# Cross-attentions: probabilities turned on four 32-row tiles in two rounds, shifting score banks, division behind the values

## The chip, the cores and the metric

The kernel runs on one core of a Trainium2 chip. The metric is device time in microseconds from launch to end of the whole decoder, the median of several executions. All matrices are float32.

## What is computed

A decoder of four layers, each with a self-attention, a cross-attention and a feed-forward part, on 8 sequences of 56 tokens with 256 features. The cross-attentions of layers 0, 2 and 3 have 16 heads and attend to a context of 1500 positions per sequence with 64 features. The part of the reference that matters here:

```python
        scores = jnp.einsum('bhsr,bhlr->bhsl', q_r, k_r)
        attn = jax.nn.softmax(scores, axis=-1)
        ctx_c = jnp.einsum('bhsl,bld->bhsd', attn, kv_r)
        ctx_lat = jnp.einsum('bhsd,hkd->bhsk', ctx_c, w_kc_kv)
        ctx = ctx_lat.transpose(0, 2, 1, 3).reshape(Bv, Sv, H * K)
        return ctx @ Wo.T
```

## The kernel before

`cross_attention` is called three times. Ahead of its loop it folds the weights so that a query has 64 features, like the context. Then it walks over `NU` = 28 units: 4 pairs of sequences (`j`) times 7 groups (`u`) of 128 rows, a row being one head of one token. A unit holds 128 rows for each sequence of the pair (`e` = 0, 1) and goes through these steps:

- **Scores** (`score(i, k)`, L1035): the 128 x 1500 scores of both sequences, in three parts of 500 columns. Sequence 0 uses rows 0 to 63 of the array, sequence 1 rows 64 to 127, so two 64-row tiles run at once. They land in PSUM banks 0 to 2 (`e` = 0) and 3 to 5 (`e` = 1). A float32 matmul is issued as two.
- **Softmax**: VectorE takes the row maxima (`rowmax`: L1315 for the three parts of sequence 0, L1320 for sequence 1 at once), ScalarE takes the exponential and the sum in one pass (`exp`, L1236), VectorE inverts the sum (L1324) and multiplies the 128 x 1500 probabilities by it in SBUF (`divide`, L1328), once per sequence.
- **Turning** (`turn(i, k)`, L1122): TensorE transposes the probabilities in blocks of 125 columns, 24 blocks a unit (12 per sequence). Each block is two transposes, of rows 0 to 63 and 64 to 127, into two banks; the block is the stationary operand, a 64 x 64 identity moves. Eight blocks fill a pair of banks; so there are three rounds `k`. The banks are those that the scores of the next unit, already exponentiated, have left, and banks 6 and 7. Two banks are copied by VectorE (L1334), four by ScalarE (L1243), 512 columns each.
- **Weighing** (`weigh(i)`, L1135): the turned probabilities times the context, summed over 12 blocks, into bank 6. VectorE copies the 128 x 128 values out (`keep`, L1341), GpSimd places them (L908).
- **Projection** (`project(j)`, L1150), after the loop.

The order on TensorE is written out: in step `i` come the scores of unit `i`, the weighing of unit `i-2`, the turning of unit `i-1`. All waits are written by hand on semaphores; every engine works its own list in order. TensorE's waits in `score` protect the banks that `turn` of the unit before last has filled and the copies have to empty (`d_in` counts VectorE's copies, `a_in` ScalarE's); those in `turn` wait for the exponentials that free the score banks (`exped`) and for the divided probabilities (`normed`).

TensorE's list, as it stands:

```python
        for i in range(1, NU):
            for k in range(3):
                score(i, k)
...
            if i >= 2:
                weigh(i - 2)
            for k in turn_order(i - 1):
                turn(i - 1, k)
```

Of the kernel before, what the change touches and what calls it, by code (L numbers as in the profile page):

```python
# [16 lines left out]
ALU = mybir.AluOpType  # L17
# [747 lines left out]
def cross_attention(c, name, o, rope, now, prefetch):  # L765
# [5 lines left out]
    s.y, s.turn_at, s.idle_bank, s.order = [(0, 0), (0, 1), (1, 0), (4, 0)], (2, 3, 5, 7), 6, range(J)  # L771
# [13 lines left out]
    else:  # L785
# [20 lines left out]
    pT = [c.at(o["PT"] + i * LT * 256, LT * 256, LP).rearrange("p (r s q) -> p r s q", r=2, q=64) for i in range(2)]  # L806
    probs = [[c.at(o["P"] + (2 * i + e) * L, L) for e in range(2)] for i in range(2)]
    held = [c.at(o["RB"] + 128 * i, 128) for i in range(2)]
    low, total, inv = (c.sb_small[:, 8 * n:8 * n + 8].rearrange("p (i e) -> p i e", e=2) for n in range(3))
    peak = c.sb_small[:, 24:36].rearrange("p (i k) -> p i k", k=3)  # L810
    sc = [c.ps[:, 3 * e:3 * e + 3, 0:4 * LP] for e in range(2)]
# [5 lines left out]
    scored, lowered, exped, recip, normed = (  # L817
        [s.sem(x + "_%d" % e) for e in range(2)] for x in ("scored", "lowered", "exped", "recip", "normed"))
    maxed, turned_lo, turned_hi, d_in, a_in, pv_mm, kept, ct_in, ct_last = (
        s.sem(x) for x in ("maxed", "turned_lo", "turned_hi", "d_in", "a_in", "pv_mm", "kept", "ct_in", "ct_last"))  # L820
# [8 lines left out]
    def turn_bank(i, k, r):  # L829
# [16 lines left out]
    def score_order(i):  # L846

        return (2, 1, 0) if i == 0 else (0, 1, 2)

    def turn_order(i):  # L850

        return (2, 0, 1) if i == 0 else (0, 1, 2)
# [37 lines left out]
    def _(pool):  # L890
# [21 lines left out]
    def _(pe):  # L912
# [108 lines left out]
        def score(i, k):  # L1021

            if i == 0 and k < 2:
                pe.wait_ge(cm_act.handle, cm_act.at(2 - k))
            if i > 0 and k == 0:
                for e in range(2):
                    pe.wait_ge(exped[e].handle, exped[e].at(i))
            if i > 1 and k < 2:
                pe.wait_ge(d_in.handle, d_in.at(2 * (i - 2) + 1 + k))
            if i > 1 and k == 2:  # L1030
                pe.wait_ge(a_in.handle, a_in.at(4 * (i - 2) + 3))
            j, u = i // UNITS, i % UNITS
            q = q2[:, j, :, :].rearrange("p h t -> p (h t)")[:, u * 128:(u + 1) * 128]
            for e in range(2):
                m = nc.tensor.matmul(sc[e][:, k, :], q[e * 64:(e + 1) * 64],  # L1035
# [4 lines left out]
                elif k == score_order(i)[-1]:  # L1040
                    m.then_inc(*scored[1].next())

        if rope:
# [22 lines left out]
            for k in score_order(0):  # L1066
                if k == 0:
                    pe.wait_ge(prod3_in.handle, prod3_in.at(3 * NH // 2))
                score(0, k)
            third(NH // 2 - 1)  # L1070
        else:
            for t in range(8):
# [17 lines left out]
                if t == 6:  # L1090
# [5 lines left out]
                    for k in score_order(0):  # L1096
                        score(0, k)
# [6 lines left out]
        def turn(i, k):  # L1104

            if k == turn_order(i)[0]:
                for e in range(2):
                    pe.wait_ge(normed[e].handle, normed[e].at(i + 1))
            if k == 0 and i < NU - 1:
                pe.wait_ge(exped[0].handle, exped[0].at(i + 2))  # L1110
            if k == 2 and i > 0:
                pe.wait_ge(kept.handle, kept.at(i))
            if i == 0 and k == 2:
                pe.wait_ge(lat_in.handle, lat_in.at(4 * NH // 2))
                pe.wait_ge(cm_act.handle, cm_act.at(3))
            if k == (1 if i == 0 else 2) and i < NU - 1:
                pe.wait_ge(exped[1].handle, exped[1].at(i + 2))
            for n in range(8):
                e, l = divmod(8 * k + n, LT)
                for r in range(2):  # L1120
                    rows = slice(r * 64, (r + 1) * 64)
                    m = nc.tensor.transpose(c.ps[0:LP, turn_bank(i, k, r), n * 64:(n + 1) * 64],  # L1122
                                            probs[i % 2][e][rows, l * LP:(l + 1) * LP], c.ident[rows, rows])
                    if n == 7:
                        m.then_inc(*(turned_hi if r else turned_lo).next())

        def weigh(i):

            j, u = i // UNITS, i % UNITS
            pe.wait_ge(a_in.handle, a_in.at(4 * (i + 1)))  # L1130
            pe.wait_ge(d_in.handle, d_in.at(2 * (i + 1)))
            y = c.ps[:, 6, :]
            for l in range(LT):
                for r, e, lo, hi in parts(u):
                    m = nc.tensor.matmul(y[r * 64:(r + 1) * 64, lo:hi], c.ctx_pos[:, j, l, e, :],  # L1135
                                         pT[i % 2][:, lo // 64:hi // 64, LT * e + l, :], start=(l == 0 and lo == 0),
# [18 lines left out]
        for i in range(1, NU):  # L1155
            for k in range(3):
                score(i, k)
            if i == 1:

                pe.wait_ge(cm_act.handle, cm_act.at(3))  # L1160
                keep_busy(c, 6, 1)
                keep_busy(c, 6, 1, None, 256)
            if i >= 2:
                weigh(i - 2)
            for k in turn_order(i - 1):
                turn(i - 1, k)
        pe.wait_ge(d_in.handle, d_in.at(2 * (NU - 1)))
# [3 lines left out]
        for k in range(3):  # L1171
            turn(NU - 1, k)
# [13 lines left out]
    def _(act):  # L1186
# [45 lines left out]
        def exp(i, e):  # L1232
            act.wait_ge(lowered[e].handle, lowered[e].at(i + 1))
            if i == 0 and not rope:
                act.wait_ge(wide_in.handle, wide_in.at(4))
            nc.scalar.activation(probs[i % 2][e].rearrange("p (k l) -> p k l", k=3), sc[e],  # L1236
                                 ACT.Exp, bias=low[:, i % 4, e:e + 1],
                                 accum_out=total[:, i % 4, e:e + 1]).then_inc(*exped[e].next())

        def copy_turned(i, k, r):  # L1240
# [1774 lines left out]
```

## Time and profile before

| | |
|---|---|
| median of 3 runs | 1663.95 us (1662.07 to 1665.45) |
| the profiled execution, its span | 1666.3 us |
| TensorE matmuls busy | 1627.4 us, 98% |
| VectorE busy | 1113.9 us, 67% |
| ScalarE busy | 749.9 us, 45% |
| GpSimd busy | 239.1 us, 14% |

In the profile PE is TensorE's matmuls and PEld its weight loads, which overlap; DVE is VectorE, ACT ScalarE, POOL GpSimd. L1122 is line 1122 of the kernel. The three unit loops lie at 205 to 456, 827 to 1077 and 1336 to 1586 us of the span. A matmul's recorded duration contains its way through the array, so several overlap; the distance between starts is what one costs.

### The profile page before, as it was taken

What the parts mean: (1) busy time and instruction counts of PE and PEld (TensorE: products, weight loads), DVE (VectorE), ACT (ScalarE), POOL (GpSimd) and SP (SyncE); (2) the same over time, 40 slices, a digit from 0 to 9 for tenths busy, and PEclk for the clock granted to TensorE, in tenths of its full rate; (3) what the DMA queues carried; (4) which work ended last, traced back from release to release, by engine and by line L of the source; (5) the groups of instructions that cost most, each with busy time, mean ns of one, the idle gap of its engine ahead of it and who ended that gap; (6) DMA issues with size and microseconds to landing.
All of it is one profiled execution on the core that took longest, in us unless ns stands there. A gap on an engine that the chain in (4) does not pass through costs nothing.

```text
span 1666.3 us, 35653 instructions
## 1 busy us (share of the span) xinstructions
PE 1627.4 (98%) x15234; PEld 1104.8 (66%) x15234; DVE 1113.9 (67%) x1974; ACT 749.9 (45%) x1297; POOL 239.1 (14%) x428
## 2 busy tenths in 40 slices
PE   9999999999999899999999999999999999999998
PEld 5575367777755666655377777764566767777765
DVE  3735899999566763266899999435445289999623
ACT  2223366666413641144366666312444366666411
POOL 0011300000010313011200000010455000000030
PEclk9999999999999999999999999999999999999999
DMA  8302020000040011051020000050300220000010
GB/s 280 86 13 83 1 78 2 2 2 2 2 187 1 2 59 40 1 133 48 1 97 2 2 2 2 4 240 0 64 1 1 114 89 2 2 2 2 2 44 11
DMA packets 35522, 71.10 MB, mean 43 GB/s; under 512 B 25359, under 2 KB 29775, under 8 KB 31433
## 3 DMA queue, kind: packets, MB, share of 16 engines
q1 hardware_dynamic: 35240, 68.71, 12.6%
q8 instruction: 121, 1.98, 0.5%
q14 instruction: 35, 0.29, 0.1%
q10 hardware_dynamic: 126, 0.11, 0.0%
HBM read 68.36 MB, written 0.46 MB: 41 GB/s over the span
## 4 chain that ended last, share of the span: by engine, by line
PE 89%; DVE 6%; ACT 2%; POOL 1%; issue 1%; DMA 1%; SPq 0%; DVEq 0%; POOLq 0%; ACTq 0%
PE ps L1122 14%; PE ps L1135 14%; PE ps L1035 13%; PE ps L1501 9%; PE ps L361 9%; PE ps L946 3%; PE ps L2599 3%; PE ps L1150 3%; PE ps L528 2%; PE ps L1961 2%; PE ps L956 1%; POOL arena L1795 1%; PE ps L2626 1%; PE ps L982 1%; PE ps L967 1%
## 5 line engine op out<-in xcount | busy, mean ns | idle before, releaser
L1236 ACT ACTIVATE arena<-ps,softmax_stats 128x1500 f32<-128x1500 f32 x168 | 253.8, 1511 | 193.0 <-DVE softmax_stats L1317 190.8
L1135 PEld LDWEIGHTS ps<-arena,ctx_pos 125*64 125x64 f32 x4608 | 222.3, 137 | 58.4 <-issue 55.4
L1122 PE MATMUL ps<-ident,arena 64*125 64x64 f32 x4032 | 239.1, 271 | 1.9 <-ACT arena L1236 1.6
L1135 PE MATMUL ps<-arena,ctx_pos 125*64 125x128 f32 (+1 forms) x4608 | 240.5, 262 | 0.0
L1122 PEld LDWEIGHTS ps<-ident,arena 64*125 64x125 f32 x4032 | 226.8, 185 | 17.0 <-issue 13.5
L1035 PE MATMUL ps<-ctx_feat,arena 64*128 64x500 f32 x1008 | 230.5, 590 | 0.0
L1243 ACT COPY arena<-ps 125x512 f32<-125x512 f32 x336 | 172.5, 600 | 77.9 <-PE ps L1122 77.9
L1315 DVE TENSOR_REDUCE softmax_stats<-ps 128x1 f32<-128x500 f32 x252 | 170.6, 678 | 49.0 <-PE ps L1035 48.6
L361 PE MATMUL ps<-arena 128*128 128x256 f32 x736 | 174.7, 383 | 3.5 <-DVE arena L1630 1.2
L1328 DVE TENSOR_SCALAR arena<-arena,softmax_stats 128x1500 f32<-128x1500 f32 x168 | 168.3, 1002 | 5.9
L1501 PE MATMUL ps<-x_feat,arena 128*128 128x448 f32 (+1 forms) x416 | 167.9, 549 | 1.2 <-DVE arena L1613 1.2
L361 PEld LDWEIGHTS ps<-arena 128*128 128x128 f32 x736 | 137.0, 190 | 40.9 <-issue 16.6
L908 POOL COPY arena<-arena 64x128 f32<-64x128 f32 (+1 forms) x186 | 51.1, 275 | 682.6 <-DVE arena L1341 676.5
L1320 DVE TENSOR_REDUCE softmax_stats<-ps 128x1 f32<-128x1500 f32 x84 | 143.6, 1709 | 0.0
L1035 PEld LDWEIGHTS ps<-ctx_feat,arena 64*128 64x128 f32 x1008 | 89.2, 187 | 80.0 <-issue 77.1
L1501 PEld LDWEIGHTS ps<-x_feat,arena 128*128 128x128 f32 (+1 forms) x416 | 79.3, 193 | 65.7 <-issue 61.7
L1334 DVE COPY arena<-ps 125x512 f32<-125x512 f32 x168 | 107.6, 682 | 12.8 <-PE ps L1122 12.5
L1577 ACT ACTIVATE arena<-ps 128x448 f32<-128x448 f32 (+1 forms) x52 | 28.2, 543 | 187.0 <-PE ps L1501 187.0
L1613 DVE TENSOR_TENSOR arena<-ps,arena 128x448 f32<-128x448 f32 x41 | 25.6, 624 | 115.6 <-ACT arena L1577 87.9
L946 PE MATMUL ps<-x_feat,arena 128*128 128x448 f32 x128 | 56.1, 563 | 0.2
L2599 PE MATMUL ps<-x_feat,arena 128*128 128x448 f32 x128 | 52.4, 552 | 1.2 <-issue 0.7
L2727 DVE TENSOR_TENSOR arena<-ps,arena 128x448 f32<-128x448 f32 x32 | 20.0, 625 | 46.0 <-ACT arena L2671 45.9
(324 smaller groups left out, 1931.7 us busy)
## 6 DMA issues: line engine op xcount, KB each, us to landing
ctx_pos<-in_ctx SPq DMA_DIRECT2D x1, 2688.0 KB
arena<-in_L1f_gate SPq DMA_DIRECT2D x1, 2304.0 KB, 12.1
arena<-in_L1f_up SPq DMA_DIRECT2D x1, 2304.0 KB, 17.0
arena<-in_L1f_down SPq DMA_DIRECT2D x1, 2304.0 KB, 7.8
arena<-in_L0a_Wq SPq DMA_DIRECT2D x1, 2048.0 KB, 10.9
arena<-in_L0a_Wc SPq DMA_DIRECT2D x1, 2048.0 KB, 18.8
arena<-in_L0x_Wq SPq DMA_DIRECT2D x1, 2048.0 KB, 9.9
arena<-in_L0x_Wo SPq DMA_DIRECT2D x1, 2048.0 KB, 8.3
```

The lines of the kernel that those rows point to most:

```text
L361: m = c.nc.tensor.matmul(y_of(c, s, j), lhsT, rhs, start=False, stop=last, skip_group_check=True)
L946: m = nc.tensor.matmul(c.ps[:, 2 + h % 2, 0:NT], wq[:, k, h, :], c.x_feat[:, k, :, 0:T], start=(k == 0), stop=(k == KT - 1))
L1035: m = nc.tensor.matmul(sc[e][:, k, :], q[e * 64:(e + 1) * 64], c.ctx_feat[e * 64:(e + 1) * 64, j, k * 4 * LP:(k + 1) * 4 * LP], start=True ...
L1122: m = nc.tensor.transpose(c.ps[0:LP, turn_bank(i, k, r), n * 64:(n + 1) * 64], probs[i % 2][e][rows, l * LP:(l + 1) * LP], c.ident[rows, r ...
L1135: m = nc.tensor.matmul(y[r * 64:(r + 1) * 64, lo:hi], c.ctx_pos[:, j, l, e, :], pT[i % 2][:, lo // 64:hi // 64, LT * e + l, :], start=(l = ...
L1236: nc.scalar.activation(probs[i % 2][e].rearrange("p (k l) -> p k l", k=3), sc[e], ACT.Exp, bias=low[:, i % 4, e:e + 1], accum_out=total[:, ...
L1243: nc.scalar.copy(pT[i % 2][:, r, 8 * k:8 * k + 8, :], c.ps[0:LP, turn_bank(i, k, r), :].rearrange("p (s q) -> p s q", s=8)).then_inc(*a_in ...
L1315: nc.vector.tensor_reduce(peak[:, i % 4, k:k + 1], sc[0][:, k, :], AX.X, ALU.max).then_inc(*maxed.next())
L1320: nc.vector.tensor_reduce(low[:, i % 4, 1:2], sc[1], AX.XY, ALU.max, negate=True).then_inc(*lowered[1].next())
L1328: nc.vector.tensor_scalar(probs[i % 2][e], probs[i % 2][e], inv[:, i % 4, e:e + 1], None, ALU.mult).then_inc(*normed[e].next())
L1334: nc.vector.tensor_copy(pT[i % 2][:, r, 0:8, :], c.ps[0:LP, turn_bank(i, 0, r), :].rearrange("p (s q) -> p s q", s=8)).then_inc(*d_in.next())
L1501: m = nc.tensor.matmul(c.ps[0:m_, bank(n) + i, 0:NT], w[:, k, n * 128:n * 128 + m_], c.x_feat[:, k, :, 0:T], start=(k == 0), stop=(k == KT ...
```

## The change

- **Turning**: for units 1 to 26 all 24 blocks go as four transposes of 32 rows each, into four banks (32 columns a block). Round 0 has 16 blocks (four banks of 512 columns), round 1 has 8 (four of 256). Unit 0 keeps 64-row tiles in three rounds; the last unit has a round of 16 blocks on four tiles and one of 8 on two. VectorE copies two banks of round 0 and one of round 1, ScalarE the other two and three.
- **Banks**: the scores of sequence 1 lie in banks 3 to 5 for even units and 4 to 6 for odd ones, their order within the unit changes, and the values go to bank 7. The waits in `score` follow the new copies.
- **Division**: the probabilities aren't divided. GpSimd spreads the two inverses of a row over 128 columns (`widen`), TensorE transposes that into a spare bank ahead of weighing (`spread_inverse`; for the middle unit of seven four small matmuls), ScalarE copies it out (`copy_inverse`), and VectorE multiplies by it where it copied the values before (`keep`, `keep_last`).

The core of the diff:

```diff
-    pT = [c.at(o["PT"] + i * LT * 256, LT * 256, LP).rearrange("p (r s q) -> p r s q", r=2, q=64) for i in range(2)]
+    pT = [c.at(o["PT"] + i * LT * 256, LT * 256, LP).rearrange("p (s q) -> p s q", q=128) for i in range(2)]
...
+    def first_bank(i, e):
+        return (3 + i % 2) * e
...
+    def spare(i):
+        return 6 if i % 2 == 0 else 3
+    def rounds(i):
         if i == 0:
-            return ((0, 1), (2, 5), (6, 7))[k][r]
+            return [(0, 8, (3, VALUES)), (8, 8, (0, 1)), (16, 8, (2, 6))]
         if i == NU - 1:
-            return ((2, 3), (4, 7), (6, 5))[k][r]
-        return ((0, 1), (2, 7), (6, 5))[k][r]
+            return [(0, 16, (2, 3, 5, 6)), (16, 8, (4, VALUES))]
+        if i % 2 == 0:
+            return [(0, 16, (0, 3, 1, 2)), (16, 8, (4, 5, VALUES, 6))]
+        return [(0, 16, (0, 6, 1, 2)), (16, 8, (4, 5, VALUES, 3))]
+    def inv_bank(i):
+        return spare(i + 2) if i + 2 < NU else 4
...
+        def widen(i):
+            pool.wait_ge(recip.handle, recip.at(i + 1))
+            nc.gpsimd.tensor_copy(wide_inv[i % 2].rearrange("p (s d) -> p s d", s=2),
+                                  inv[:, i % 4, :].unsqueeze(2).broadcast_to([128, 2, 64])).then_inc(*widened.next())
+        widen(0)
         for i in range(NU - 1):
+            if i > 0:
+                pool.wait_ge(ct_in.handle, ct_in.at(placed(i - 1)))
+            widen(i + 1)
+            pool.wait_ge(widened.handle, widened.at(i + 2))
...
-            if i > 0 and k == 0:
+        def score(i, n):
+            if i == 0 and n > 0:
+                pe.wait_ge(cm_act.handle, cm_act.at(n))
+            if i > 0 and n == 0:
                 for e in range(2):
                     pe.wait_ge(exped[e].handle, exped[e].at(i))
-            if i > 1 and k < 2:
-                pe.wait_ge(d_in.handle, d_in.at(2 * (i - 2) + 1 + k))
-            if i > 1 and k == 2:
-                pe.wait_ge(a_in.handle, a_in.at(4 * (i - 2) + 3))
+            if i == 1 and n == 2:
+                pe.wait_ge(cm_act.handle, cm_act.at(3))
+            if i == 2 and n < 2:
+                pe.wait_ge(d_in.handle, d_in.at(d_at(0, n + 1)))
+            if i == 2 and n == 2:
+                pe.wait_ge(a_in.handle, a_in.at(a_at(0, 3)))
+            if i > 2:
+                pe.wait_ge(d_in.handle, d_in.at(d_at(i - 2, (1, 3, 3)[n])))
+                pe.wait_ge(a_in.handle, a_in.at(a_at(i - 2, (1, 1, 3)[n])))
...
+        def turn(i, n):
+            if i == 0 and n == 0:
+                pe.wait_ge(lat_in.handle, lat_in.at(4 * NH // 2))
+            if i < NU - 1 and n == (1 if i == 0 else 0):
                 pe.wait_ge(exped[0].handle, exped[0].at(i + 2))
-            if k == 2 and i > 0:
+            if i > 0 and n == 0:
+                pe.wait_ge(inv_in.handle, inv_in.at(i))
+            if i > 0 and n == 1:
                 pe.wait_ge(kept.handle, kept.at(i))
-            if i == 0 and k == 2:
-                pe.wait_ge(lat_in.handle, lat_in.at(4 * NH // 2))
-                pe.wait_ge(cm_act.handle, cm_act.at(3))
-            if k == (1 if i == 0 else 2) and i < NU - 1:
+            if i < NU - 1 and n == len(rounds(i)) - 1:
                 pe.wait_ge(exped[1].handle, exped[1].at(i + 2))
-            for n in range(8):
-                e, l = divmod(8 * k + n, LT)
-                for r in range(2):
-                    rows = slice(r * 64, (r + 1) * 64)
-                    m = nc.tensor.transpose(c.ps[0:LP, turn_bank(i, k, r), n * 64:(n + 1) * 64],
+            block, blocks, banks = rounds(i)[n]
+            w = 128 // len(banks)
+            for m in range(blocks):
+                e, l = divmod(block + m, LT)
+                for t, bank in enumerate(banks):
+                    rows = slice(t * w, (t + 1) * w)
+                    x = nc.tensor.transpose(c.ps[0:LP, bank, m * w:(m + 1) * w],
                                             probs[i % 2][e][rows, l * LP:(l + 1) * LP], c.ident[rows, rows])
-                    if n == 7:
-                        m.then_inc(*(turned_hi if r else turned_lo).next())
+                    if m == blocks - 1:
+                        x.then_inc(*turned[t].next())
+        def spread_inverse(i):
+            u = i % UNITS
+            pe.wait_ge(widened.handle, widened.at(i + 1))
+            if u == SPLIT:
+                for r, e, lo, hi in parts(u):
+                    m = nc.tensor.matmul(c.ps[r * 64:(r + 1) * 64, inv_bank(i), lo:hi], inv[:, i % 4, e:e + 1].broadcast_to([128, 64]),
+                                         c.ident[:, lo:hi], start=True, stop=True, skip_group_check=True)
+            else:
+                m = nc.tensor.transpose(c.ps[:, inv_bank(i), 0:128], wide_inv[i % 2], c.ident[:])
+            m.then_inc(*inv_mm.next())
...
+            pe.wait_ge(a_in.handle, a_in.at(a_at(i, a_copies(i))))
+            pe.wait_ge(d_in.handle, d_in.at(d_at(i, d_copies(i))))
+            spread_inverse(i)
...
+                copy_inverse(i - 2)
             if i < NU:
                 exp(i, 0)
                 exp(i, 1)
             if i == 0:
                 cm_out(3)
                 place(7)
-            if i >= 1:
-                copy_turned(i - 1, 1, 0)
-                copy_turned(i - 1, 1, 1)
-                copy_turned(i - 1, 2, 1)
-                copy_turned(i - 1, 2, 0)
+            if i == 1:
+                copy_turned(0, 0, 0)
+                copy_turned(0, 0, 1)
+                copy_turned(0, 2, 0)
+                copy_turned(0, 2, 1)
+            if i >= 2:
+                copy_turned(i - 1, 0, 1)
+                copy_turned(i - 1, 0, 3)
+                if i < NU:
+                    copy_turned(i - 1, 1, 1)
+                    copy_turned(i - 1, 1, 2)
+                    copy_turned(i - 1, 1, 3)
...
-        def divide(i, e):
-            dve.wait_ge(recip[e].handle, recip[e].at(i + 1))
-            nc.vector.tensor_scalar(probs[i % 2][e], probs[i % 2][e], inv[:, i % 4, e:e + 1], None,
-                                    ALU.mult).then_inc(*normed[e].next())
...
+            nc.vector.tensor_tensor(held[i % 2], c.ps[:, VALUES, 0:128], spread[i % 2], ALU.mult).then_inc(*kept.next())
...
+                copy_turned(i - 1, 0, 0)
+                copy_turned(i - 1, 0, 2)
+                if i < NU:
+                    copy_turned(i - 1, 1, 0)
             if i < NU:
-                normalise(i, 1)
+                invert(i)
```

## Rows read from the trace of the kernel before

**Rows 1.** The page: span, busy times of two engines, the turning's group.

```profile
span 1666.3 us, 35653 instructions
...
PE 1627.4 (98%) x15234; PEld 1104.8 (66%) x15234; DVE 1113.9 (67%) x1974; ACT 749.9 (45%) x1297; POOL 239.1 (14%) x428
...
L1122 PE MATMUL ps<-ident,arena 64*125 64x64 f32 x4032 | 239.1, 271 | 1.9 <-ACT arena L1236 1.6
```

**Rows 2.** The page: lines of the chain that ended last, share of the span.

```profile
PE ps L1122 14%; PE ps L1135 14%; PE ps L1035 13%; PE ps L1501 9%; PE ps L361 9%; PE ps L946 3%; PE ps L2599 3%; PE ps L1150 3%; PE ps L528 2%; PE ps L1961 2%; PE ps L956 1%; POOL arena L1795 1%; PE ps L2626 1%; PE ps L982 1%; PE ps L967 1%
```

**Rows 3.** Busy times by engine inside the first loop; columns in the first line.

```profile
core 0: us, PE busy (x) PEld busy (x) DVE busy (x) ACT busy (x) POOL busy (x), PEclk, DMA share, GB/s
300.00:400.00 100.00, 100.00 (x1432) 78.08 (x1432) 91.94 (x150) 64.93 (x101) 8.23 (x30) 1.00 0.01 2
```

**Rows 4.** Order of time, one unit: start us, us; then engine, line, operation, count.

```profile
334.35 2.73 PE L1035 MATMUL ps<-ctx_feat,arena 64*128 64x500 f32 x12
...
337.01 2.60 PEld L1135 LDWEIGHTS ps<-arena,ctx_pos 125*64 125x64 f32 x48 [0.74 <-issue]
...
339.43 0.19 ACT L1236 ACTIVATION_READ_ACCUMULATOR arena<-ps,softmax_stats 128x1 f32 x1
...
339.78 2.69 PEld L1122 LDWEIGHTS ps<-ident,arena 64*125 64x125 f32 x48 [0.17 <-issue]
...
340.97 1.28 DVE L1334 COPY arena<-ps 125x512 f32<-125x512 f32 x2
...
341.77 2.05 ACT L1243 COPY arena<-ps 125x512 f32<-125x512 f32 x4 [0.53 <-PE ps L1122]
...
342.39 0.30 PEld L1035 LDWEIGHTS ps<-ctx_feat,arena 64*128 64x128 f32 x4
342.45 2.73 PE L1035 MATMUL ps<-ctx_feat,arena 64*128 64x500 f32 x12
```

**Rows 5.** Order of time, TensorE: the unit's last pair of score matmuls.

```profile
336.50 0.58 PE L1035 MATMUL ps<-ctx_feat,arena 64*128 64x500 f32 x2
```

**Rows 6.** Single lines, weight loads: duration ns minimum/median/maximum; shape.

```profile
L967 PEld LDWEIGHTS ps<-arena x128: 106/108/109, 149.4 to 822.7; 128*32 128x32 f32 x128
...
L924 PEld LDWEIGHTS ps<-arena x192: 156/162/162, 142.4 to 1304.6; 64*96 64x96 f32 x192
...
L1122 PEld LDWEIGHTS ps<-ident,arena x4032: 180/186/186, 216.6 to 1574.8; 64*125 64x125 f32 x192
...
L2626 PEld LDWEIGHTS ps<-arena x256: 182/188/188, 1194.4 to 1294.6; 56*128 56x128 f32 x128
...
L1839 PEld LDWEIGHTS ps<-ident,arena x128: 137/141/143, 546.3 to 749.6; 128*128 128x128 f32 x128
```

**Rows 7.** Order of time, weight loads: four 32-row tiles of the last self-attention.

```profile
1146.94 0.20 PEld L2552 LDWEIGHTS ps<-arena 32*128 32x128 f32 x3 [0.81 <-issue]
1146.96 0.18 PEld L2556 LDWEIGHTS ps<-arena 32*128 32x128 f32 x1
1147.05 0.20 PEld L2552 LDWEIGHTS ps<-arena 32*128 32x128 f32 x3
```

**Rows 8.** Order of time, weight loads: two whole-array transposes, then column tiles.

```profile
1192.80 0.20 PEld L2617 LDWEIGHTS ps<-ident,arena 128*128 128x128 f32 x2 [0.69 <-DVE arena L2749]
1193.16 0.55 PEld L2608 LDWEIGHTS ps<-arena 128*64 128x64 f32 x16 [0.17 <-issue]
```

**Rows 9.** Groups at 300 to 400 us: busy us, mean ns of one, idle before.

```profile
L1328 DVE TENSOR_SCALAR arena<-arena,softmax_stats 128x1500 f32<-128x1500 f32 x26 | 26.0, 1002 | 0.9
...
L1334 DVE COPY arena<-ps 125x512 f32<-125x512 f32 x26 | 16.6, 682 | 0.1
...
L908 POOL COPY arena<-arena 64x128 f32<-64x128 f32 x22 | 6.4, 290 | 82.2 <-DVE arena L1341 81.6
...
L1341 DVE COPY arena<-ps 128x128 f32<-128x128 f32 x13 | 3.7, 284 | 0.0
```

**Rows 10.** Order of time, weight loads: 32-row tiles of another self-attention.

```profile
539.58 0.91 PEld L1825 LDWEIGHTS ps<-arena 32*64 32x64 f32 x64 [0.65 <-issue]
```

More of the change, by code:

```diff
@@ L770, in cross_attention @@
     s.summed, s.groups, s.by_act = False, [range(0, 3), range(3, 4)], [0, 1]
-    s.y, s.turn_at, s.idle_bank, s.order = [(0, 0), (0, 1), (1, 0), (4, 0)], (2, 3, 5, 7), 6, range(J)
+    s.y, s.turn_at, s.idle_bank, s.order = [(0, 0), (0, 1), (1, 0), (4, 0)], (2, 3, 5, 6), 7, range(J)
     if rope:
@@ L816, in cross_attention @@
         s.sem(x) for x in ("big2_mm", "big3_mm", "prod2_in", "prod3_in", "rot2_in", "rot3_in"))
[L817 to L820, printed above, removed]
+    scored, lowered, exped = (
+        [s.sem(x + "_%d" % e) for e in range(2)] for x in ("scored", "lowered", "exped"))
+    turned = [s.sem("turned_%d" % t) for t in range(4)]
+    maxed, recip, widened, inv_mm, inv_in, d_in, a_in, pv_mm, kept, ct_in, ct_last = (
+        s.sem(x) for x in ("maxed", "recip", "widened", "inv_mm", "inv_in", "d_in", "a_in", "pv_mm", "kept", "ct_in", "ct_last"))
     cm_mm, padded = s.sem("cm_mm"), s.sem("padded")
@@ L823, in cross_attention, with half, score_banks, d_at @@
     NU = J * UNITS
-    def turn_bank(i, k, r):
+    def first_bank(i, e):
+        return (3 + i % 2) * e
+    def half(i, e):
+        return 1 - e if i % UNITS > SPLIT else e
+    def score_banks(i, e):
+        return c.ps[:, first_bank(i, e):first_bank(i, e) + 3, 0:4 * LP]
+    VALUES = 7
+    def spare(i):
+        return 6 if i % 2 == 0 else 3
+    def rounds(i):
         if i == 0:
-            return ((0, 1), (2, 5), (6, 7))[k][r]
+            return [(0, 8, (3, VALUES)), (8, 8, (0, 1)), (16, 8, (2, 6))]
         if i == NU - 1:
-            return ((2, 3), (4, 7), (6, 5))[k][r]
-        return ((0, 1), (2, 7), (6, 5))[k][r]
+            return [(0, 16, (2, 3, 5, 6)), (16, 8, (4, VALUES))]
[4 more added lines that the diff above has]
+        return spare(i + 2) if i + 2 < NU else 4
+    def d_at(i, n):
+        return (2 + 3 * (i - 1) if i else 0) + n
+    def a_at(i, n):
+        return (4 + 5 * (i - 1) if i else 0) + n
+    def d_copies(i):
+        return 2 if i in (0, NU - 1) else 3
+    def a_copies(i):
+        return 4 if i in (0, NU - 1) else 5
+    def turned_out(i, n, t):
+        block, blocks, banks = rounds(i)[n]
+        w = 128 // len(banks)
+        return (pT[i % 2][:, block:block + blocks, t * w:(t + 1) * w],
+                c.ps[0:LP, banks[t], 0:blocks * w].rearrange("p (s q) -> p s q", s=blocks))
+    def turned_at(i, n, t):
+        if t < 2:
+            return (3 + 2 * (i - 1) if i else 0) + n + 1
+        return 2 * (i - 1) + n + 1
     def wide_bank(g, r):
@@ L1065, in _ @@
             pe.wait_ge(lat_in.handle, lat_in.at(4 * 6))
-            for k in score_order(0):
-                if k == 0:
+            for n in range(3):
+                if n == 2:
                     pe.wait_ge(prod3_in.handle, prod3_in.at(3 * NH // 2))
-                score(0, k)
+                score(0, n)
             third(NH // 2 - 1)
@@ L1095, in _ @@
                     pe.wait_ge(lat_in.handle, lat_in.at(4 * 6))
-                    for k in score_order(0):
-                        score(0, k)
+                    for n in range(3):
+                        score(0, n)
                 if 3 <= t <= 6:
@@ L1135, in weigh @@
                     m = nc.tensor.matmul(y[r * 64:(r + 1) * 64, lo:hi], c.ctx_pos[:, j, l, e, :],
[L1136 removed]
+                                         pT[i % 2][:, LT * e + l, lo:hi], start=(l == 0 and lo == 0),
                                          stop=(l == LT - 1), skip_group_check=True)
@@ L1155, in _ @@
         for i in range(1, NU):
-            for k in range(3):
-                score(i, k)
+            for n in range(3):
+                score(i, n)
             if i == 1:
-                pe.wait_ge(cm_act.handle, cm_act.at(3))
-                keep_busy(c, 6, 1)
-                keep_busy(c, 6, 1, None, 256)
+                pe.wait_ge(lat_in.handle, lat_in.at(4 * NH // 2))
+                keep_busy(c, VALUES, 1)
+                keep_busy(c, VALUES, 1, None, 256)
             if i >= 2:
                 weigh(i - 2)
-            for k in turn_order(i - 1):
-                turn(i - 1, k)
-        pe.wait_ge(d_in.handle, d_in.at(2 * (NU - 1)))
+            for n in range(len(rounds(i - 1))):
+                turn(i - 1, n)
+        pe.wait_ge(d_in.handle, d_in.at(d_at(NU - 2, 1)))
         project(0)
@@ L1170, in _ @@
         project(1)
-        for k in range(3):
-            turn(NU - 1, k)
+        for n in range(2):
+            turn(NU - 1, n)
         project(2)
```

94 lines of the change are left out of this document (48 added, 46 removed).

## The prediction

> **What bounds the kernel now.** I read the page's first part and its groups, then the chain, then one stretch of steady work, then one unit in order of time. The page shows TensorE busy for 1627.4 of 1666.3 us, and VectorE, the next one, for 1113.9 [rows 1]. The chain that ended last runs over TensorE, and its three largest lines, 41% of the span together, are those that the change touches: turning the probabilities (L1122), weighing the context (L1135), the scores (L1035) [rows 2]. In a stretch that lies wholly inside the unit loop TensorE is busy 100.00 of 100 us, VectorE 91.94, ScalarE 64.93, at a granted clock of 1.00 [rows 3].
>
> One unit shows why. A unit's scores begin at 334.35 and the next one's at 342.45: the period is 8.10 us [rows 4]. In between TensorE weighs from 337.01, turns from 339.78 and is back at score loads at 342.39. The reader is to see that none of these starts waits for data. The first exponential, which the turn needs, has its sum written at 339.43 + 0.19 = 339.62, 0.16 us before the turn starts. The short pause ahead of weighing is the engine's own: weighing steps by (2.60 - 0.14) / 23 = 0.107 us per 128 moving columns (24 pairs of loads in 2.60 us [rows 4], one lasting 0.135 to 0.14 by the line of rows 6), so the last score pair's 500 columns take 0.42; it starts at 336.50 [rows 5], the array is free at 336.92, and the next load starts at 337.01. I call that 0.09 us, seen where the array changes its tiling, a switch. So the unit's period is TensorE's own sum, and work taken from VectorE or ScalarE gives nothing unless TensorE waited for it.
>
> **What sets the pace of turning.** 48 weight loads reach over 2.69 us from first start to last end [rows 4], one lasting 0.186 [rows 6]: (2.69 - 0.186) / 23 = 0.109 us per pair, and 24 x 0.109 = 2.62 us is the whole turn. Is that the loads, or the moving of the 64 identity columns? Load durations lie on one line: 32 columns 108 ns, 96 columns 162, 125 columns 186, 128 columns 188 [rows 6], so 0.84 ns a column, whatever the rows (128, 64, 64, 56). 125 columns stream for some 105 ns, which is the step of 109 less 4. The loads set the pace; the 64 moving columns (some 53 ns by the weighing's pace) fit inside. One form is off the line: 128 columns of a whole-array transpose load in 141 ns [rows 6].
>
> **The change, part by part.**
>
> 1. *Turning on four 32-row tiles.* The 24 blocks of 125 columns stay; each is loaded four times with 32 rows instead of twice with 64, and moves 32 columns instead of 64. What was short becomes shorter; what bounds stays, if a 32-row load takes as long and four run side by side. The nearest rows are the four 32-row tiles of the last self-attention: four loads of 128 columns start within 20 ns, last 0.18 each, and the next four start 0.11 us after the first [rows 7]. Taken: 24 x 0.109 = 2.62, change 0. Bound above: two more issues a block, at most 7 ns each as in rows 7, add 24 x 0.014 = 0.34 if nothing hides them; a gain is the first rival.
>
> 2. *Going back to the scores.* Both were 64-row tiles and followed each other without a switch (339.78 + 24 x 0.109 = 342.40, loads at 342.39 [rows 4]). Now 32-row tiles are followed by 64-row ones. If that is a switch, the next load waits for the last 32 columns (27 ns) and 0.09: +0.12 us. Bounds 0 and 0.12; I take 0.12, since the changes of tiling on either side of weighing are switches in the same rows.
>
> [...]
>
> 3. *Spreading the inverse.* Between scores and weighing comes one 128 x 128 transpose on the whole array. The nearest rows are two such ones followed by column tiles: from the first load to the next tiling's load 1193.16 - 1192.80 = 0.36 us [rows 8]. One less (0.107 for 128 moving columns) leaves 0.255 us per unit. Bounds 0.18 (half) and 0.36. In the middle unit of every seven it is four small matmuls in the weighing's own tiling; I count the same.
>
> 4. *Division.* Two multiplies of 1.00 us leave VectorE per unit; a multiply takes the place of the 128-column copy (0.284) [rows 9]. GpSimd gets a broadcast copy (nearest row 0.29 for 64 partitions [rows 9]); it stands behind a wait for the placing of the unit before and ahead of the wait for the kept values, and has a unit's time and more. ScalarE gets a 128-column copy ahead of both exponentials; its transpose ends before the first row maximum is complete, so it is hidden there. All of this lies beside TensorE. Gain on the path: 0, since TensorE didn't wait for the divided values.
>
> 5. *Two rounds and the copies.* The first round is 16 blocks, so its copies start 15 x 0.109 + 0.33 = 1.97 us after the turn does (now ScalarE's start at 341.77, 0.36 after the sixteenth pair's load [rows 4]; 27 ns less for 32 columns). VectorE then copies two tiles of 512 columns, 1.28 [rows 4], and one of 256, between 0.28 and 0.68 [rows 9], on a straight line 0.42: done at 3.58, the copies overlapping a little. The scores start at 2.62 + 0.12 = 2.74. Their second third wants its loads at 3.57 but waits for that third copy until about 3.62: +0.05 us. Bounds 0 and 0.3 (0.68 for that copy, or pieces of 32 columns written slowly). ScalarE's five copies keep ahead of what waits for them.
>
> **Sum.** A steady unit grows by 0.12 + 0.255 + 0.05 = 0.42 us, to 8.52. Per attention: 25 returns to the scores x 0.17 = 4.25; 28 inverses x 0.255 = 7.1; two of these stand behind a projection that had no switch to the weighing before, and the last unit turns on 32-row and then 64-row tiles, 0.5 together. That is 11.9, and 35.6 for three attentions. The profiled execution took 1666.3, 2.35 more than the median of the runs, 1663.95. So 1666.3 + 35.6 - 2.35 = 1699.5; I say **1699**. The ends: with 0.18 for the inverse alone 3 x 28 x 0.18 = 15, so 1679; with all bounds, and half of the issue's 0.34, 25 x (0.12 + 0.3 + 0.17) + 28 x 0.36 + 0.5 = 25.3 per attention, so 1740.
>
> **Rivals.**
>
> *Turning becomes faster.* If 32-row tiles loaded faster, the turn would shrink until issue binds: 64 loads of 32-row tiles reach over 0.91 us [rows 10], 14 ns each and up to 66 for four with what they wait for. At 66 the turn takes 1.58 instead of 2.62, but then the copies decide: VectorE's three end at 1.32 + 1.20 + 0.42 = 2.94, the scores start at 2.04 and lose 0.10 in the middle, and with the inverse's 0.255 the period is 7.88, 0.22 less. 25 x 0.22 x 3 less some 2 at the ends: **1649**. It decides from about 87 ns per block down. For it: the whole-array transpose shows that a load can be shorter, 141 ns. Against it: the present transposes in tiles, 186 ns, don't have that, and no load of fewer rows is shorter than the line.
>
> [...]
>
> *The four tiles share what two use now.* Then a block takes 0.22 and a unit 2.6 us more: 26 x 2.6 x 3 = 203 above the forecast, **1900**. Against it: rows 7.
>
> *It cancels.* The inverse is partly hidden and blocks step at 90 to 100 ns: **1655 to 1679**.
>
> *The change doesn't do what it says,* relieve VectorE to shorten units, or rather it does and VectorE was the bound. For it: 91.94 of 100 us. Against it: TensorE was busy for all of those 100 us, and in the whole span L1122 stood idle for 1.9 us [rows 1], which is all that earlier values could give: **1697**, inside the forecast.
>
> **How the numbers follow.** Forecast 0.77, faster turning 0.11, cancelling 0.08, sharing 0.04. The forecast's own range is 1679 to 1740; with most of the cancelling case 1658 to 1740 leaves out about 2 in 10. About 0.2%, 3.3 us, is what a measurement of this kernel can tell from no change. Of the cancelling case half is within that, a quarter on either side: faster 0.13, same 0.04, slower 0.83.
>
> **What would show it.** In the changed profile 32-row loads of 125 columns should last 0.186, and a unit's 96 should reach over 2.7 us; a unit should take 8.5 us; VectorE should fall to some three quarters in steady work while TensorE stays at all of it; between scores and weighing 0.25 us more should lie, with one load in it. Loads of 32 rows much shorter than 0.186, or blocks stepping under 90 ns, would prove me wrong, and so would turns that start as soon as an exponential ends, which would mean that the path isn't TensorE's.

## The result, and the profile after

The changed kernel takes **1791.5 us** (median of four runs, 1791.1 to 1793.5) against 1664.4 for the kernel before on the same chip: a ratio of 1.074, 95% interval 1.070 to 1.077. It is slower, as forecast, but by 127 us where I had worked out 36; 1791.5 lies outside my range of 1658 to 1740. The profiled execution has a span of 1789.9 us, 123.6 more than the one of before [rows 1].

The page of the changed kernel, its parts 1, 2 and 5 (group columns: busy us, mean ns of one, idle before):

```profile
span 1789.9 us, 44209 instructions
...
PE 1741.9 (97%) x19242; PEld 1162.1 (65%) x19242; DVE 972.3 (54%) x1800; ACT 760.6 (42%) x1459; POOL 264.2 (15%) x512
...
PEclk9999989889899999999988988999999989889899
...
L1104 PE MATMUL ps<-ctx_feat,arena 64*128 64x500 f32 x1008 | 316.8, 774 | 7.9 <-issue 0.3
...
L1191 PE MATMUL ps<-ident,arena 32*125 32x32 f32 (+1 forms) x7872 | 237.8, 269 | 1.9 <-ACT arena L1318 1.6
L1191 PEld LDWEIGHTS ps<-ident,arena 32*125 32x125 f32 (+1 forms) x7872 | 227.4, 184 | 17.1 <-issue 13.5
```

VectorE has lost 142 us of work, and TensorE is as busy as before. The turning, now L1191, costs what it cost: 237.8 us here, 239.1 in [rows 1]. Two things don't fit my prediction. The row of the granted clock has eights in all three stretches where the cross-attentions run. And the group that grew is the scores (L1104): the change gives them other banks and waits, but leaves their matmuls as they are. Their group on the page of before:

```profile
L1035 PE MATMUL ps<-ctx_feat,arena 64*128 64x500 f32 x1008 | 230.5, 590 | 0.0
```

The single line shows how they grew, first in the kernel before, then in the changed one (duration ns minimum/median/maximum):

```profile
L1035 PE MATMUL ps<-ctx_feat,arena x1008: 579/579/683, 205.1 to 1556.6; 64*128 64x500 f32 x168
```

```profile
L1104 PE MATMUL ps<-ctx_feat,arena x1008: 579/654/1200, 202.3 to 1678.7; 64*128 64x500 f32 x168
```

The same matmul on the same tiles now lasts up to 1200 ns. Windows on the first cross-attention of the changed kernel (the first line names the columns; a stretch of five units, one of 90 us, the turning of one unit, the scores behind that turning, and the first part of these scores):

```profile
core 0: us, PE busy (x) PEld busy (x) DVE busy (x) ACT busy (x) POOL busy (x), PEclk, DMA share, GB/s
253.50:297.00 43.50, 42.90 (x833) 33.34 (x831) 28.99 (x51) 26.96 (x51) 4.72 (x17) 1.00 0.01 2
310.00:400.00 90.00, 89.08 (x1503) 64.61 (x1501) 51.38 (x90) 46.91 (x89) 8.57 (x31) 0.85 0.01 2
...
371.94:374.83 2.89, 2.81 (x98) 2.70 (x97) 1.21 (x3) 2.09 (x4) 0.58 (x2) 0.98 0.00 0
374.83:379.17 4.34, 4.31 (x12) 1.84 (x12) 2.13 (x5) 1.01 (x4) 0.29 (x1) 0.62 0.01 4
374.83:378.20 3.37, 3.34 (x8) 1.63 (x10) 1.45 (x4) 1.01 (x4) 0.29 (x1) 0.51 0.02 5
```

In [rows 3] the clock was 1.00, and in the trace of before it doesn't fall anywhere in the unit loops (1.00 over each of the three). Here it is 1.00 from 253.5 to 297 and 0.85 from 310 to 400: about when a turning ends it falls from 1.00 to half (0.51 in the last row, 0.50 from 375.00 to 378.00), between 0.2 us ahead of the first score load and 0.8 behind it, and the scores that follow take 4.34 us. Such a drop and the stretch at half the clock behind it, 3.4 us in the trace's clock records, is called a fall below. PE's busy column shows nothing of this: 4.31 of 4.34.

Weight loads in order of time, first in units at full clock, then in a unit with a fall (start us, us; in brackets the idle time before):

```profile
270.42 0.14 PEld L1205 LDWEIGHTS ps<-ident,arena 128*128 128x128 f32 x1 [0.74 <-issue]
270.68 2.60 PEld L1217 LDWEIGHTS ps<-arena,ctx_pos 125*64 125x64 f32 x48
273.44 2.70 PEld L1191 LDWEIGHTS ps<-ident,arena 32*125 32x125 f32 x96 [0.17 <-issue]
276.33 0.33 PEld L1104 LDWEIGHTS ps<-ctx_feat,arena 64*128 64x128 f32 x4 [0.18 <-issue]
277.08 0.41 PEld L1104 LDWEIGHTS ps<-ctx_feat,arena 64*128 64x128 f32 x4 [0.43 <-DVE arena L1427]
...
279.07 0.14 PEld L1205 LDWEIGHTS ps<-ident,arena 128*128 128x128 f32 x1 [0.74 <-issue]
...
284.99 0.33 PEld L1104 LDWEIGHTS ps<-ctx_feat,arena 64*128 64x128 f32 x4 [0.18 <-issue]
...
371.94 2.70 PEld L1191 LDWEIGHTS ps<-ident,arena 32*125 32x125 f32 x96 [0.17 <-issue]
374.83 0.53 PEld L1104 LDWEIGHTS ps<-ctx_feat,arena 64*128 64x128 f32 x4 [0.18 <-issue]
...
379.17 0.14 PEld L1205 LDWEIGHTS ps<-ident,arena 128*128 128x128 f32 x1 [0.74 <-issue]
```

At full clock the period is 284.99 - 276.33 = 8.66 us; I had 8.52. The slow unit's scores reach the next inverse after 4.34 us, where the fast one needs 279.07 - 276.33 = 2.74.

**Where the 123.6 us lie.** The three attentions have 81 distances from one unit's first score load to the next one's. They add up to 656.0 us before and 776.5 after, so 120.5 of the 123.6 are there. In the changed kernel's trace 48 falls of the clock lie in them. Units without a fall have a median of 8.66 us, units with one 10.35. At 8.66 throughout, the 81 would take 701.5. So **45.5 us** come from longer units (81 x 0.56) and **75.0 us** from the clock, 1.56 for each fall. The falls add up to 163.8 us at a granted clock of 0.50, and half of that, 82, would be lost if TensorE worked through all of it. The two figures agree nearly; the 75.0 is what is left over 81 units at the median, so it is good to a few us.

### The profile page after: what moved, and what is told of

It is laid out like the page before. It is cut to its first block, busy times and chain, and to the rows that moved or that the text cites. A ratio compares the mean times of both kernels' runs of the same rounds, so it can differ in the third digit from the quotient of the medians.

```text
span 1789.9 us, 44209 instructions
## 1 busy us (share of the span) xinstructions
PE 1741.9 (97%) x19242; PEld 1162.1 (65%) x19242; DVE 972.3 (54%) x1800; ACT 760.6 (42%) x1459; POOL 264.2 (15%) x512
## 4 chain that ended last, share of the span: by engine, by line
PE 89%; DVE 5%; ACT 2%; issue 2%; POOL 1%; DVEq 0%; POOLq 0%; ACTq 0%
PE ps L1104 18%; PE ps L1191 13%; PE ps L1217 13%; PE ps L361 9%; PE ps L1595 8%; PE ps L1009 3%; PE ps L2693 3%; PE ps L1232 3%; PE ps L528 2%; PE ps L2055 2%; PE ps L1019 1%; PE ps L1205 1%; POOL arena L1889 1%; PE ps L2720 1%; PE ps L1045 1%
## 5 line engine op out<-in xcount | busy, mean ns | idle before, releaser
L1104 PE MATMUL ps<-ctx_feat,arena 64*128 64x500 f32 x1008 | 316.8, 774 | 7.9 <-issue 0.3
L1191 PE MATMUL ps<-ident,arena 32*125 32x32 f32 (+1 forms) x7872 | 237.8, 269 | 1.9 <-ACT arena L1318 1.6
L1191 PEld LDWEIGHTS ps<-ident,arena 32*125 32x125 f32 (+1 forms) x7872 | 227.4, 184 | 17.1 <-issue 13.5
L1104 PEld LDWEIGHTS ps<-ctx_feat,arena 64*128 64x128 f32 x1008 | 132.5, 248 | 129.5 <-issue 95.1
L1427 DVE COPY arena<-ps 125x512 f32<-125x512 f32 (+1 forms) x246 | 134.1, 600 | 134.5 <-PE ps L1191 134.5
L1324 ACT COPY arena<-ps 125x256 f32<-125x256 f32 (+1 forms) x414 | 161.1, 483 | 89.7 <-PE ps L1191 89.7
L1328 ACT COPY arena<-ps 128x128 f32<-128x128 f32 x84 | 22.4, 266 | 267.2 <-PE ps L1205 220.8
L958 POOL COPY arena<-softmax_stats 128x128 f32<-128x128 f32 x84 | 24.4, 290 | 267.3 <-DVE softmax_stats L1423 267.3
L1434 DVE TENSOR_TENSOR arena<-ps,arena 128x128 f32<-128x128 f32 x81 | 23.6, 292 | 72.8 <-issue 69.0
L1009 PE MATMUL ps<-x_feat,arena 128*128 128x448 f32 x128 | 56.1, 563 | 0.2
```

The costliest lines, as they stand in the source:

```text
L1009: m = nc.tensor.matmul(c.ps[:, 2 + h % 2, 0:NT], wq[:, k, h, :], c.x_feat[:, k, :, 0:T], start=(k == 0), stop=(k == KT - 1))
L1104: m = nc.tensor.matmul(c.ps[:, first_bank(i, e) + k, 0:4 * LP], q[e * 64:(e + 1) * 64], c.ctx_feat[e * 64:(e + 1) * 64, j, k * 4 * LP:(k + ...
L1191: x = nc.tensor.transpose(c.ps[0:LP, bank, m * w:(m + 1) * w], probs[i % 2][e][rows, l * LP:(l + 1) * LP], c.ident[rows, rows])
L1324: nc.scalar.copy(*turned_out(i, n, t)).then_inc(*a_in.next())
L1427: nc.vector.tensor_copy(*turned_out(i, n, t)).then_inc(*d_in.next())
```

## The experiments

The theory to be tested was that turning on 32-row tiles leaves TensorE so little at work that the clock falls. The rivals put the lost time into what the change does besides: the division with its whole-array transpose, the shifted banks, the two rounds. The ratios are to the kernel before, timed again beside them (medians 1667.5 and 1667.3 us). Falls are counted in the profiled execution, in the 81 distances.

### The tile height alone: two 64-row tiles in the new frame

In `turn` of the changed kernel, with the copies' addresses to match:

```diff
-            w = 128 // len(banks)
+            tiles = min(len(banks), 2)
+            w, share = 128 // tiles, blocks * tiles // len(banks)
...
-                for t, bank in enumerate(banks):
-                    rows = slice(t * w, (t + 1) * w)
-                    x = nc.tensor.transpose(c.ps[0:LP, bank, m * w:(m + 1) * w],
+                for t in range(tiles):
+                    rows, g = slice(t * w, (t + 1) * w), m // share * tiles + t
+                    x = nc.tensor.transpose(c.ps[0:LP, banks[g], m % share * w:(m % share + 1) * w],
```

> The changed kernel with its four banks, two rounds, shifting score banks and division at the exit all kept, but the turning on two 64-row tiles: the first half of a round's blocks goes to two of the banks, the second half to the other two. 48 transposes of 64 columns in place of 96 of 32. [...] Rival (the time lies in the division, the shifted banks and the rounds, which are all still there): 1775 to 1795 us.

By the theory I had put 1690 to 1715 us here, with a mean granted clock of 0.985 or more: 78 us less than the changed kernel, and 0.12 us a unit less for the tile switch ahead of the scores. The 78 is what the clock had taken: 0.949 granted over 1789.9 us leaves 91 us missing, 0.992 over 1666.3 leaves 13.

It took **1686.9 us**, ratio 1.012 (1.008 to 1.015), mean granted clock 0.996. A window inside the loop, and the loads at the end of one turning:

```profile
300.00:400.00 100.00, 100.00 (x1412) 77.09 (x1409) 70.22 (x120) 65.30 (x119) 11.11 (x40) 1.00 0.01 2
```

```profile
375.87 2.69 PEld L1195 LDWEIGHTS ps<-ident,arena 64*125 64x125 f32 x48 [0.17 <-issue]
378.49 0.30 PEld L1107 LDWEIGHTS ps<-ctx_feat,arena 64*128 64x128 f32 x4
```

The turning takes the same 2.69 us of loads, and only 3 falls are left in the 81 distances, all three in the second unit of a loop, ahead of the first turning whose form the edit changes. Of the 127 us, 105 hang on the tile height: 97 lie in the 81 distances (776.5 against 679.6 us), and the rest fits falls outside the loops, where the clock was down for 21 us in the changed kernel's profile and for 5 here. It came out 3 us below what I expected mainly because not only the tile switch went but a wait for copies too: the scores' loads start before the last turning load has ended.

### The same frame with whole-array transposes

The edit is the one above with `tiles = min(len(banks), 1)`: each block's 128 rows in one transpose.

> The changed kernel with the same banks and rounds, but the turning by whole-array transposes: each block's 128 rows in one, a quarter of a round's blocks to each bank. 24 transposes of 128 columns in place of 96 of 32. Theory: the step stays 0.109 us for a block, the clock stays up (as with 64-row tiles), and the switch ahead of the scores stays: 1695 to 1725 us, mean granted clock 0.985 or more. Rival (banks, rounds and division): 1775 to 1795 us.

It took **1702.2 us**, ratio 1.019 (1.016 to 1.023), clock 0.995, as expected, with no fall in the loops. Its line of loads (duration ns minimum/median/maximum), and the loads of one turning in order of time:

```profile
L1195 PEld LDWEIGHTS ps<-ident,arena x2016: 183/188/188, 213.3 to 1610.1; 128*125 128x125 f32 x184
```

```profile
377.80 2.69 PEld L1195 LDWEIGHTS ps<-ident,arena 128*125 128x125 f32 x24 [0.17 <-issue]
380.61 0.30 PEld L1107 LDWEIGHTS ps<-ctx_feat,arena 64*128 64x128 f32 x4
```

24, 48 or 96 transposes: the turning's loads reach over 2.69 to 2.70 us in all three forms. A load of 125 columns lasts 188 ns on the whole array too (the 141 of [rows 6] is another line's, with 128 columns). What a block cost here didn't depend on its tiles. Here the scores' loads start 380.61 - 380.49 = 0.12 us after the last load ends, with 64-row tiles 0.07 us before it ends. So the switch from the whole array to 64-row tiles costs 0.19 us, and the period is 8.56 in place of 8.36.

### The division alone, in the kernel before

The largest of its edits: TensorE spreads the inverse ahead of weighing, VectorE multiplies the values, and the multiplies of the probabilities go.

```diff
+            spread_inverse(i)
             y = c.ps[:, 6, :]
...
-            nc.vector.tensor_copy(held[i % 2], c.ps[:, 6, 0:128]).then_inc(*kept.next())
+            nc.vector.tensor_tensor(held[i % 2], c.ps[:, 6, 0:128], spread[i % 2], ALU.mult).then_inc(*kept.next())
...
-                normalise(i, 0)
...
-                normalise(i, 1)
+                invert(i)
```

> The kernel before with one part of the change alone: the division leaves the probabilities and is made where the values leave PSUM, with the transpose that spreads the reciprocals (bank 7, free at that point), its copy by ScalarE and the widening by GpSimd. Score banks, 64-row tiles and three rounds stay as they were. Theory: the division costs TensorE's 0.26 us a unit and nothing else, 18 to 22 us, and the shifted banks with two rounds nothing: 1682 to 1692 us, the same as the kernel with the changed banks on 64-row tiles. Rival (the shifted banks and rounds carry a part of what that kernel loses): under 1678 us here. The prediction's fifth case, where VectorE bounds the unit, would show a gain here: under 1664 us.

It took **1687.0 us**, ratio 1.012 (1.006 to 1.017), clock 0.996. The first loop's window, to be held against [rows 3], and one unit's loads:

```profile
300.00:400.00 100.00, 100.00 (x1410) 77.10 (x1408) 65.07 (x108) 65.65 (x107) 11.19 (x40) 1.00 0.01 2
```

```profile
378.55 0.30 PEld L1054 LDWEIGHTS ps<-ctx_feat,arena 64*128 64x128 f32 x4
...
381.27 0.14 PEld L1157 LDWEIGHTS ps<-ident,arena 128*128 128x128 f32 x1 [0.74 <-issue]
381.53 2.60 PEld L1169 LDWEIGHTS ps<-arena,ctx_pos 125*64 125x64 f32 x48
```

VectorE falls from 91.94 to 65.07 of 100 us and the kernel gets slower: the inverse puts 381.53 - 381.27 = 0.26 us on TensorE's path, the period goes from 8.10 to 8.36. This is the same time and the same period as the new frame on 64-row tiles. So the shifted banks and the two rounds cost nothing there, and the case of VectorE as the bound has fallen.

### The changed kernel without the inverse

Values leave PSUM undivided: the transpose of the inverse, its copy and the multiplication are left out.

```diff
-            spread_inverse(i)
             y = c.ps[:, VALUES, :]
...
-            if i >= 2:
-                copy_inverse(i - 2)
```

> The changed kernel without the transpose that spreads the reciprocals, its copy, its waits and the multiplication: the values leave PSUM undivided. The turning on 32-row tiles stays. Theory: 0.26 us a unit goes, some 21 us, and the clock still falls after the turning: 1755 to 1780 us, mean granted clock 0.93 to 0.96. Rival (the one whole-array transpose in the middle of column-tiled and row-tiled work lets the clock fall): clock 0.985 or more and 1680 to 1700 us.

It took **1762.3 us**, ratio 1.055 (1.051 to 1.058), clock 0.955, as expected: 29 us less than the changed kernel, and 35 falls in the loops are left. So the clock falls without the whole-array transpose too; why 13 times less often, this run doesn't tell.

### Work added between the rounds: one matmul of 512 columns

```diff
+            if 0 < i < NU - 1 and n == 1:
+                keep_busy(c, 4, 1)
```

> The changed kernel with one more matmul in each unit, between the two rounds of the turning: 128 rows by 512 columns of no use, into a bank that the second round then overwrites. Nothing is taken away. Theory (the granted clock falls because the turning is too light): the matmul and the two changes of tile cost up to 0.45 us a unit, 35 us over the units, and the fall of the clock goes, 78 us: 1730 to 1765 us, mean granted clock 0.985 or more. Rival (the added time is stalls, or the clock has nothing to do with the turning): the work adds its 35 us, 1810 to 1835 us, clock 0.95.

It took **1790.4 us**, ratio 1.072 (1.069 to 1.076), clock **0.996**. Neither time came true. The clock did what the theory says: 2 falls are left in the loops, both in a loop's second unit, where the matmul hasn't yet been added. But the matmul cost more than all I had put down for it:

```profile
371.70 1.83 PEld L1193 LDWEIGHTS ps<-ident,arena 32*125 32x125 f32 x64 [0.17 <-issue]
373.56 0.30 PEld L170 LDWEIGHTS ps<-ctx_feat,ident 128*128 128x128 f32 x2
374.62 0.95 PEld L1193 LDWEIGHTS ps<-ident,arena 32*125 32x125 f32 x32 [0.76 <-issue]
375.62 0.30 PEld L1104 LDWEIGHTS ps<-ctx_feat,arena 64*128 64x128 f32 x4
```

The turning now reaches over 375.57 - 371.70 = 3.87 us in place of 2.70. A float32 matmul is issued as two (x2), each of 512 columns, and on either side TensorE changes its tiling. The period is 9.66 at full clock, 1.00 more, and 78 us of added work (26 units in each of three loops) stand against 75 of returned clock. The rows give something else, though: the scores' loads start 0.05 us after the last turning load, against 276.33 - 276.14 = 0.19 in the changed kernel and -0.08 before [rows 4]. Here the copies of the first round have long ended, so the step from -0.08 to 0.05, **0.13 us**, is the switch from 32-row to 64-row tiles, and the remaining **0.14 us** of the changed kernel is a wait for copies (the section on the prediction shows which).

### Work added on the same tiles, in two sizes

```diff
+            if 0 < i < NU - 1 and n == 1:
+                for t, bank in enumerate(banks):
+                    rows = slice(t * 32, (t + 1) * 32)
+                    nc.tensor.matmul(c.ps[:, bank, 0:256], c.ident[rows, :], c.ctx_feat[rows, 0, 0:256],
+                                     start=True, stop=True, skip_group_check=True)
```

> The changed kernel with four more matmuls in each unit between the two rounds of the turning, one on each 32-row tile, 256 columns each, of no use, into the banks that the second round overwrites: work on the same tiles, so no change of tile. Theory (too little work lets the clock fall): they take 0.22 us a unit together, 17 us, the wait for the copies ahead of the scores goes (0.14 us a unit, 11 us), and the fall of the clock goes, 78 us: 1705 to 1735 us, less than the changed kernel although it does more, mean granted clock 0.985 or more. Rival (the fall has another cause): 1790 to 1810 us, clock 0.95.

> The same four added matmuls with 64 columns in place of 256: 0.05 us a unit, 4 us. If so little work holds the clock: 1700 to 1730 us, clock 0.985 or more. If the fall goes by how much work stands in the stretch, it stays in part or wholly: 1760 to 1795 us, clock 0.94 to 0.97. Theory: the second.

With 256 columns it took **1756.9 us** (1.053, 1.047 to 1.058), with 64 columns **1777.6** (1.066, 1.060 to 1.071), at mean clocks of 0.981 and 0.959. Each does all that the changed kernel does and more, and each is faster than its 1791.5; with 64 columns the intervals of the two ratios just touch (1.071 and 1.070). Falls in the loops: 48 without the added matmuls, 39 with 64 columns, 15 with 256. The smaller one came out as I expected. The larger one missed my range on two counts: not all falls go, and its turning reaches over 377.66 - 374.53 = 3.13 us of loads in place of 2.70, 0.43 more where I had 0.22 (eight loads go with its eight matmuls). Loads of the larger one in a unit at full clock:

```profile
374.53 1.83 PEld L1196 LDWEIGHTS ps<-ident,arena 32*125 32x125 f32 x64 [0.17 <-issue]
376.27 0.31 PEld L1189 LDWEIGHTS ps<-ctx_feat,ident 32*128 32x128 f32 x8
376.60 1.06 PEld L1196 LDWEIGHTS ps<-ident,arena 32*125 32x125 f32 x32
377.71 0.30 PEld L1104 LDWEIGHTS ps<-ctx_feat,arena 64*128 64x128 f32 x4
```

The distance to the scores' loads is again 377.71 - 377.66 = 0.05 us.

### The first round on 32-row tiles, the second on 64-row tiles

The edit is that of the first experiment with `tiles = min(len(banks), 4 if n == 0 else 2)`.

> The changed kernel with the first round of the turning (16 blocks) on four 32-row tiles as it is and the second (8 blocks) on two 64-row tiles, the four banks kept: a third of the light stretch goes, and the change of tile moves from ahead of the scores to between the rounds. If a turning that is light for 1.75 us in place of 2.62 still lets the clock fall: 1765 to 1795 us, clock 0.94 to 0.96. If it is the full length that does it: 1690 to 1720 us, clock 0.985 or more. Theory: the second, since the fall comes at the end of the turning.

It took **1751.0 us**, ratio 1.048 (1.044 to 1.053), clock 0.972, with 20 falls in the loops: between my two answers, and the one that I had preferred missed by more than 30 us. A shorter stretch on 32-row tiles lets the clock fall less often, not never. One unit with a fall:

```profile
372.12 2.82 PEld L1195 LDWEIGHTS ps<-ident,arena 32*125 32x125 f32 x80 [0.17 <-issue]
375.00 0.43 PEld L1107 LDWEIGHTS ps<-ctx_feat,arena 64*128 64x128 f32 x4
```

The turning ends on the scores' own tiles, so no switch stands ahead of them, and still the scores' loads start 375.00 - 374.94 = 0.06 us after the last load instead of 0.08 before it ends. That 0.14 is the wait for copies again, seen without a switch.

Two more causes can be ruled out from these runs together. The pause between turning and scores isn't what lets the clock fall: with whole-array transposes it is 0.12 us and there are no falls, with the four added matmuls of 64 columns it is 0.04 and there are 39. Nor is it the number of instructions: with the four added matmuls there are more of them on the same tiles, and fewer falls. And the counts, each from one execution, aren't chance: in the four executions of each kernel the mean clock is 0.947 to 0.951 (changed kernel), 0.954 to 0.961 (64 columns added), 0.971 to 0.974 (the two heights mixed), 0.979 to 0.981 (256 columns added) and 0.990 or more (64-row tiles, whole array).

## Why the prediction was wrong

Going through its steps:

- **What bounds the kernel: right.** The division alone took 27 of 100 us from VectorE and gave nothing. The rival in which VectorE is the bound fell with it.
- **Turning (24 x 0.109): right in its time, and the step that failed.** A 32-row load lasts 184 ns and a unit's 96 reach over 2.70 us; I had put 0.186 and 2.7. The failure is in the sentence that the 64 moving columns "fit inside". I then cut them to 32 on each tile and booked the shorter movement at nothing, because it was not what set the pace. It was not free: in the changed kernel the granted clock falls to 0.50 behind 48 turnings of this form, and behind none of these turnings when they go on two 64-row tiles or on the whole array, where their loads reach over as long (2.69 us). I read the granted clock of 1.00 in [rows 3] as a given of the kernel and carried it over. It was a property of what TensorE did, and the change altered just that. No term and no rival of mine had the clock in it; it is worth 75 us, 61% of the difference.
- **Spreading the inverse (0.255): right.** 0.26 in the rows; 676.6 - 656.0 = 20.6 us over the 81 distances of the kernel with the division alone.
- **Division beside TensorE (0): right**, by the same kernel.
- **Going back to the scores (0.12): right.** 0.13 by the kernel with the added matmul of 512 columns.
- **Copies (0.05): too small; it is 0.16.** My course of VectorE's three copies came true. In order of time, the changed kernel's VectorE behind the turning that starts at 273.44:

```profile
275.41 1.62 DVE L1427 COPY arena<-ps 125x512 f32<-125x512 f32 x3 [1.50 <-PE ps L1191]
```

  They start 1.97 us after the turning, as in the sum, and the loads of the second third follow their end at 277.03 after 0.05, at 277.08. But the first third waits too, for the first copy of each copying engine. By my own figures VectorE's ends at 1.97 + 0.68 = 2.65 us, ahead of the 2.74 at which the scores start, so I booked nothing for it; only in the rival of the faster turning did I count it (the scores at 1.32 + 0.68 + 0.04 = 2.04). The copy does end there, at 276.10. The loads start 0.23 us after it, though, not 0.05, and so 0.14 later than the switch alone would have them. The trace's records of TensorE's wait instructions show where that goes: the wait for VectorE's copy is recorded 0.04 us after the copy's end, the wait for ScalarE's, whose copy had ended 0.07 us before VectorE's, another 0.11 later, and the first load 0.08 behind it. In the kernel with 256 added columns the first of these waits also stands 0.04 us behind the copy, but the scores' loads come 0.48 us after it: there it delays nothing. From the first score load to the inverse it is 2.74 us against 381.27 - 378.55 = 2.72 with 64-row tiles. That makes 8.10 + 0.26 + 0.13 + 0.14 + 0.02 = 8.65 for the unit, where 8.66 is measured. So the longer units cost 45.5 us over the 81 distances, where I had 35.6 for all.
- **Rivals.** Faster turning didn't come: with 96, 48 or 24 transposes a block steps at 0.109 us. Tiles sharing what two used (1900) didn't come either; that the total moved part of the way there has another cause.

**What stays open.** Why the falls come in runs of units and leave out others with the same rows, as from 253.5 to 297 us, isn't told by these runs. Within a run each fall mostly starts a little earlier in its unit than the one before (0.72, 0.60, 0.33, 0.22, 0.10 us behind the first score load in one run). That suggests that the unit's length has a part in how many units are hit, so the counts of 39, 35, 20 and 15 are no measure of the added work alone. It doesn't touch the main finding: with periods of 8.10, 8.36 and 8.56 us and no turning on 32-row tiles, no steady unit has a fall.

None of the kernels beats the one before. In each that was tried TensorE's own work makes all of the period but the wait of 0.14 us, and each adds to it.

## What to carry to other kernels

When a change cuts what TensorE does inside a step whose length something else sets, the granted clock of that stretch is an unknown of the prediction, with a price to be taken from what runs behind it: here 1.56 us for each fall. Look at the clock row before the busy row, since a TensorE at half clock is shown as busy as one at full clock (4.31 of 4.34 us here). And work moved off an engine that isn't the bound pays only if none of it lands on the one that is; 0.26 us a unit did.

## What the runs showed of the hardware that I had not expected

- The granted clock fell while TensorE was shown busy for 98.98% of the stretch (89.08 of 90 us): mean clock 0.85.
- Work of no use made the kernel faster: four more matmuls a unit on the 32-row tiles, -14 us with 64 columns each and -35 us with 256.
- A 125-column block costs 0.109 us of turning in three forms: one transpose of 128 rows, two of 64 or four of 32.
- Changes of tiling were unequal: 0.13 us from 32-row to 64-row tiles, 0.19 us from the whole array to 64-row tiles.
